# Four attention blocks on one core: where the values of an earlier half stand in TensorE's order

## The chip, the cores and the metric

The kernel runs on one core of a Trainium2 chip. The time is that of the device for one execution, in microseconds (us); 374.49 us is the median of three runs of the kernel before.

## The reference

An activation `x` of 8 batches x 128 positions x 128 channels goes through four cross-attention layers one after the other, against one context of 8 x 128 x 256. Layers 0 and 3 are "narrow" (RMS norm, 16 query heads of 8 dimensions that share 4 key and value heads, no mask). Layers 1 and 2 are "wide" (16 heads of 64 dimensions, a bias on some columns). Everything is float32. Cut to a wide layer:

```python
q = hidden_states @ Wq                      # per batch 128 x 1024, 16 heads of 64
k = encoder_hidden_states @ Wk
v = encoder_hidden_states @ Wv
logits = einsum('bhqd,bhkd->bhqk', q, k) * scale + col_bias
probs = softmax(logits, axis=-1)
out = einsum('bhqk,bhkd->bhqd', probs, v)
out = out.reshape(B, HW, 1024) @ Wo + bo + hidden_states
```

## The kernel before

A **job** `n` is one layer of one batch; there are 32 (`JOBS`), in two turns of 16: four batches through layers 0, 1, 2, 3, then the other four. Jobs 4 to 11 and 20 to 27 are wide, the rest narrow. A job has two **halves** of 8 heads, `h` = 0 and 1, and all engines count halves by `o = 2n + h`; "half 50" is `o` = 50, the first half of job 25. Within a half the heads are on two sides of four heads each.

The kernel is software-pipelined over a loop of half slots. Each engine has its own program in a fixed order written out by hand, and semaphores tie them together; no scheduler moves anything. In the slot of half `o` TensorE (PE) does, in this order:

1. the **scores** of half `o` (`wide_scores`, line 834): 8 products with a 64-row contraction, two at a time on the upper and the lower 64 rows, into the banks `scores_ps`;
2. the **values** of half `o-3` (`weighted_values`, line 881): 8 products that give 64 rows each, two at a time on two column halves of the array, into `v_ps`, from the transposed probabilities `probsT`;
3. the **transposes** of the probabilities of half `o-2` (`transpose_probs`, line 847) into `pt_ps`;
4. **fills**: projections of the context into keys and values that a later job needs (`project_context`, lines 700 to 702). The table `FILLS` says which half slot has how many; slots 12 to 22, 44, 46, 48, 50, 52 and 54 have one or two, the odd slots 49 and 51 have none, slot 53 has a small one;
5. the **queries** of half `h` of the next job (`queries`, line 786) into `q_ps`, or, where the next job is narrow and `h` is 0, its mean square and queries (`narrow_queries`, lines 799 and 806), which write into `v_ps` and so wait for `v_read`, VectorE's copy of the values two jobs back out of that bank;
6. with `h` = 0 the **output projection** of job `n-2` (line 899), 8 products of the values of both its halves with `Wo`, into `v_ps` too, after the same `v_read`.

VectorE (DVE) in the slot of half `o` goes: with `h` = 1 the residual add of job `n-2` (line 633); the scores of half `o` out of PSUM with the bias and the row minimum, side 0, then side 1 (line 596), with a reciprocal between them; the values of half `o-3` out (`oT`, line 623); the transposed probabilities of half `o-2` out, both sides (`probsT`, line 616, semaphores `pt_read`); a reciprocal. ScalarE (ACT) does the exponentials of half `o` (line 476) and copies out queries and fills; GpSimd (POOL) multiplies with the reciprocals (line 376).

The values of half `o-3` wait on TensorE for `pt_read` of half `o-3` of both sides, that is for the last two copies of VectorE's slot `o-1`, and for `v_read`:

```python
if n > 0:
    pe.wait_ge(v_read, uses(n, h) - 1)
...
for side in range(2):
    pe.wait_ge(pt_read[side], o + 1)
```

Of the kernel before, what the change touches and what calls it, by code (L numbers as in the profile page):

```python
# [103 lines left out]
def job(n):  # L104

    return JOBS[n] if 0 <= n < NJOBS else (None, None)


def is_narrow(n):

    return 0 <= n < NJOBS and JOBS[n][0] in NARROW


def is_wide(n):

    return 0 <= n < NJOBS and JOBS[n][0] not in NARROW


def uses(n, h):

    return sum(2 if is_wide(m) else 1 for m in range(n)) + (h + 1 if is_wide(n) else 1)
# [29 lines left out]
def count_of(bank, use):  # L151

    return BANK_USES[bank].index(use) + 1


def narrow_index(n):

    return NARROW_JOBS.index(n)


def build(nc, xT, ctxT, narrow_w, narrow_kv, kv_w, qo_w, small, tokens, outT):
    with ExitStack() as ctx:
# [108 lines left out]
        def valid(o):  # L271

            return 0 <= o < 2 * NJOBS
# [422 lines left out]
        def _(pe):  # L696
# [81 lines left out]
            def queries(n, h):  # L778

                l, b = job(n)  # L780
                free_bank(Q0, ("queries", n, h))
                pe.wait_ge(qo_loaded[l - 1], 16)
                pe.wait_ge(y_read, JOBS.index((l - 1, b)) + 1)
                for c in range(4):
                    first = WQ + (4 * h + c) * P
                    last = nc.tensor.matmul(q_ps[:, c * T:(c + 1) * T], w_qo[:, l - 1, first:first + P], x[:, b, :],  # L786
                                            start=True, stop=True)
                last.then_inc(bank_full[Q0], 1)
# [19 lines left out]
            def narrow_scores(n):  # L808

                i = narrow_index(n)  # L810
                for r in range(REP):
                    free_bank(r, (2 * n + r // 2, r % 2))
                pe.wait_ge(kd_made, i + 1)
                pe.wait_ge(qn_made, i + 1)
                for r in range(REP):
                    rows = slice(PART * r, PART * (r + 1))
                    nc.tensor.matmul(banks[r][:], qn[rows, n % 2, :], kd[rows, i % KD_RING].rearrange("p g k -> p (g k)"),  # L817
                                     start=True, stop=True).then_inc(bank_full[r], 1)

            def wide_scores(n, h):  # L820
                o = 2 * n + h
                l, b = job(n)
                for side in range(2):
                    free_bank(side, (o, side))
                pe.wait_ge(bank_read[Q0], count_of(Q0, ("queries", n, h)))
                f = WIDE_ROWS.index((b // 2, l))
                for m in (2 * h, 2 * h + 1):
                    name = f"k{f}.{m}"
                    pe.wait_ge(bank_read[FILL_BANK[name]], count_of(FILL_BANK[name], name))

                for c in range(4):
                    for side in range(2):
                        rows = slice(side * WIDE_D, (side + 1) * WIDE_D)
                        last = nc.tensor.matmul(banks[side][:, c * S:(c + 1) * S], qT[rows, 4 * h + c, :],  # L834
                                                kT[rows, f % KV_RING, 4 * h + c, b % 2 * S:(b % 2 + 1) * S],
                                                start=True, stop=True)
                        if c == 3:
                            last.then_inc(bank_full[side], 1)

            def transpose_probs(o):  # L840
                for side in range(2):
                    pe.wait_ge(probs_made[side], o + 1)
                    if o > 0:
                        pe.wait_ge(pt_read[side], o)
                    for q in range(4):
                        cols = slice(q * S, (q + 1) * S)
                        last = nc.tensor.transpose(pt_ps[side][:, cols], probs[:, o % PROBS_RING, side, cols], identity)  # L847
                    last.then_inc(pt_full[side], 1)

            def weighted_values(n, h):  # L850
                o = 2 * n + h
                l, b = job(n)
                if l in NARROW and h == 0:
                    return
                if n > 0:
                    pe.wait_ge(v_read, uses(n, h) - 1)
                if n > 0 and (h == 0 or l in NARROW):
                    pe.wait_ge(y_read, n)
                if is_narrow((o + 4) // 2):
                    pe.wait_ge(rms_out, narrow_index((o + 4) // 2) + 1)  # L860
                    pe.wait_ge(qn_made, narrow_index((o + 4) // 2) + 1)
                for side in range(2):
                    pe.wait_ge(pt_read[side], o + 1)
                if l in NARROW:
                    i = narrow_index(n)
                    pe.wait_ge(vn_made, i + 1)
                    for g in range(KV_HEADS):
                        for r in range(REP):
                            last = nc.tensor.matmul(v_ps[PART * r:PART * (r + 1), 0:T],  # L869
                                                    v_narrow[:, i % 2, PART * g:PART * (g + 1)],  # L870
                                                    probsT[:, (o - 1 + r // 2) % PROBST_RING, r % 2, g * T:(g + 1) * T], start=(g == 0),
                                                    stop=(g == KV_HEADS - 1))
                    last.then_inc(v_full, 1)
                    return
                f = WIDE_ROWS.index((b // 2, l))
                name = f"v{f}.{2 * (b % 2) + h}"
                pe.wait_ge(bank_read[FILL_BANK[name]], count_of(FILL_BANK[name], name))
                for c in range(4):
                    for side in range(2):
                        head = 8 * h + 2 * c + side  # L880
                        last = nc.tensor.matmul(  # L881
                            v_ps[side * WIDE_D:(side + 1) * WIDE_D, c * T:(c + 1) * T],
                            v[:, f % KV_RING, b % 2, head * WIDE_D:(head + 1) * WIDE_D],
                            probsT[:, o % PROBST_RING, side, c * T:(c + 1) * T], start=True, stop=True)
                last.then_inc(v_full, 1)
# [16 lines left out]

            def half(n, h):
                o = 2 * n + h
                if is_wide(n):
                    wide_scores(n, h)
                if is_narrow(n) and h == 0:
                    narrow_scores(n)
                if o == 0:
                    warm_up(3)  # L910
                if o >= FIRST_WAIT and valid(o - 2) and o - 2 != LAST:
                    pe.wait_ge(bank_read[Q0], len(BANK_USES[Q0]))
                    warm_up(4, q_ps)
                if valid(o - 3) and is_wide((o - 3) // 2):
                    weighted_values((o - 3) // 2, (o - 3) % 2)
                if valid(o - 2) and o - 2 != LAST:
                    transpose_probs(o - 2)
                if valid(o - 3) and is_narrow((o - 3) // 2):
                    weighted_values((o - 3) // 2, (o - 3) % 2)
                names = [name for name, bank in FILLS.get(o, [])]  # L920
                behind = names[1:] if h == 0 and is_narrow(n) and is_narrow(n + 1) else []
                for name in names[:len(names) - len(behind)]:
                    project_context(name)
                if is_wide(n + 1):
                    queries(n + 1, h)
                if h == 0 and is_narrow(n + 1):
                    narrow_queries(n + 1)
                if o - 1 == LAST:
                    transpose_probs(LAST)
                if h == 0 and n >= 2:  # L930
                    output_projection(n - 2)
                for name in behind:
                    project_context(name)

            def warm_up(count, bank=pt_ps[0]):

                for _ in range(count):
                    nc.tensor.matmul(bank[:, 0:T], mean_w[:], mean_w[:], start=True, stop=True)  # L938
# [8 lines left out]
            for n, h in HALVES:  # L947
                half(n, h)
# [59 lines left out]
```

## Time and profile before

| | |
|---|---|
| median of 3 runs | 374.49 us (374.46 to 374.75) |
| the profiled execution's own time | 374.53 us |
| its span, first to last instruction | 372.7 us |
| busy: TensorE, ScalarE, VectorE, GpSimd | 358.1, 280.1, 249.1, 178.7 us |
| mean granted TensorE clock | 0.986 of full speed |

The span is 1.8 us shorter than the profiled execution's time. Weight loads (PEld) and matmuls (PE) are shown apart. A float32 matmul stands as two instructions in the trace, so that the 8 products of the scores or the values of a half are x16, and the 4 of the queries x8; a transpose stands as two too, 4 on a side. A matmul's end is modelled and pipelined with the next one's start, so starts are compared with starts here.

### The profile page before, as it was taken

To read this page: it belongs to the slowest core of one execution; us is meant where nothing else is said; L and a number is where in the kernel's file an instruction comes from. 1 tells how busy PE (TensorE), PEld (TensorE's weight loads), DVE (VectorE), ACT (ScalarE), POOL (GpSimd) and SP (SyncE) were. 2 spreads that over 40 slices of the span, in tenths; PEclk is the share of its full clock that TensorE was granted. 3 is DMA by queue.
4 is the path that set the end of the run, shared out by engine and by line. 5 is a ranking of instruction groups with operands and counts; after the bars stand their busy time and mean duration, and the time that the engine had idled before them with its cause. 6 is when DMAs were issued, how large, how long until landed. Compare 5 with 4: busy or idle time off the path is not lost.

```text
span 372.7 us, 10531 instructions
## 1 busy us (share of the span) xinstructions
PE 358.1 (96%) x3552; PEld 311.1 (83%) x3552; DVE 249.1 (67%) x1385; ACT 280.1 (75%) x1176; POOL 178.7 (48%) x205
## 2 busy tenths in 40 slices
PE   8897999999999999999999999999999999988985
PEld 7776779889989989978887878988999999866874
DVE  2899675365465466579677777556647666689884
ACT  4897897865755756576899999987667666676893
POOL 3696643552332334265667665433233424456761
PEclk9897899999999999999999999999999999999999
DMA  7943000000000000000000000000000000000000
GB/s 229 409 144 139 0 4 3 2 1 2 3 2 0 3 2 2 1 2 3 2 11 7 9 11 2 3 2 2 2 2 3 3 0 3 2 3 0 3 9 21
DMA packets 4883, 9.71 MB, mean 26 GB/s; under 512 B 608, under 2 KB 3296, under 8 KB 4576
## 3 DMA queue, kind: packets, MB, share of 16 engines
q1 hardware_dynamic: 4400, 8.65, 6.5%
q8 instruction: 29, 0.48, 0.5%
q10 hardware_dynamic: 432, 0.40, 0.4%
q14 instruction: 22, 0.18, 0.2%
HBM read 8.53 MB, written 0.52 MB: 24 GB/s over the span
## 4 chain that ended last, share of the span: by engine, by line
PE 86%; DVE 10%; ACT 2%; issue 1%; POOL 0%; DVEq 0%; POOLq 0%
PE pt_ps L847 14%; PE scores_ps L834 9%; PE v_ps L899 9%; PE v_ps L881 8%; PE q_ps L786 7%; DVE probs L596 5%; PE fill_ps L700 5%; PE fill_ps L701 5%; PE fill_ps L702 5%; PE v_ps L869 4%; PE scores_ps L817 4%; PE scores_ps L700 3%; PE scores_ps L702 2%; PE scores_ps L701 2%; PE pt_ps L938 1%; PE q_ps L700 1%
## 5 line engine op out<-in xcount | busy, mean ns | idle before, releaser
L476 ACT ACTIVATE probs<-probs,negmax 128x128 f32<-128x128 f32 x512 | 198.4, 390 | 64.8 <-DVE negmax L596 64.5
L376 POOL TENSOR_TENSOR probs<-probs,inv 128x512 f32<-128x512 f32 x127 | 135.1, 1063 | 178.0 <-DVE inv L603 177.8
L476 ACT ACTIVATION_READ_ACCUMULATOR probs<-probs,negmax 128x1 f32 x512 | 96.8, 189 | 0.0
L596 DVE CUSTOM_DVE_ANT_0 probs<-scores_ps,col_bias 128x128 f32<-128x128 f32 x256 | 58.2, 283 | 39.3 <-PE scores_ps L834 39.3
L847 PE MATMUL pt_ps<-smalls,probs 128*128 128x128 f32 x512 | 69.6, 279 | 0.7 <-DVE probsT L616 0.7
L847 PEld LDWEIGHTS pt_ps<-smalls,probs 128*128 128x128 f32 x512 | 56.2, 142 | 15.2 <-issue 12.4
L616 DVE COPY probsT<-pt_ps 128x512 f32<-128x512 f32 x96 | 62.7, 680 | 2.7 <-PE pt_ps L847 2.6
L596 DVE CUSTOM_DVE_ANT_0 probs<-scores_ps,no_bias,inv_rms 128x128 f32<-128x128 f32 x128 | 36.7, 342 | 12.9 <-PE scores_ps L817 12.9
L596 DVE DVE_READ_ACCUMULATOR2_ANT negmax<- 128x1 f32 x512 | 41.9, 82 | 0.0
L834 PE MATMUL scores_ps<-kT,qT 64*128 64x128 f32 x512 | 37.2, 285 | 0.0
L596 DVE CUSTOM_DVE_ANT_0 probs<-fill_ps,no_bias,inv_rms 128x128 f32<-128x128 f32 x128 | 36.4, 339 | 0.0
L881 PE MATMUL v_ps<-probsT,v 128*64 128x128 f32 x512 | 35.0, 279 | 1.0 <-DVE rms L573 1.0
L834 PEld LDWEIGHTS scores_ps<-kT,qT 64*128 64x128 f32 x512 | 31.1, 187 | 3.9
L786 PE MATMUL q_ps<-x,w_qo 128*128 128x128 f32 x256 | 33.8, 275 | 0.0
L786 PEld LDWEIGHTS q_ps<-x,w_qo 128*128 128x128 f32 x256 | 32.0, 191 | 1.3 <-issue 0.2
L881 PEld LDWEIGHTS v_ps<-probsT,v 128*64 128x64 f32 x512 | 27.3, 136 | 6.8 <-issue 3.4
L899 PE MATMUL v_ps<-oT,w_qo 128*128 128x128 f32 x256 | 31.2, 275 | 0.0
L633 DVE SCALAR_TENSOR_TENSOR x<-v_ps,smalls,x 128x128 f32<-128x128 f32 x16 | 5.6, 350 | 36.5 <-PE v_ps L899 36.5
L899 PEld LDWEIGHTS v_ps<-oT,w_qo 128*128 128x128 f32 x256 | 29.9, 192 | 0.0
L603 DVE RECIPROCAL inv<-rowsum 128x4 f32<-128x4 f32 x128 | 21.9, 171 | 11.6 <-ACT probs L476 11.6
L467 ACT ACTIVATE qT<-q_ps 128x512 f32<-128x512 f32 x32 | 18.7, 586 | 9.0 <-PE q_ps L786 9.0
L623 DVE COPY oT<-v_ps 128x512 f32<-128x512 f32 x32 | 21.9, 685 | 0.0
(146 smaller groups left out, 642.6 us busy)
## 6 DMA issues: line engine op xcount, KB each, us to landing
kT<-in_kv_w SPq DMA_DIRECT2D x6, 512.0 KB, 6.2
w_qo<-in_qo_w SPq DMA_DIRECT2D x2, 1024.0 KB, 8.2
v<-in_ctxT SPq DMA_DIRECT2D x4, 256.0 KB, 9.2
v<-in_kv_w SPq DMA_DIRECT2D x2, 512.0 KB, 10.8
outT<-x SPq DMA_DIRECT2D x8, 64.0 KB, 1.6
x<-in_xT SPq DMA_DIRECT2D x1, 384.0 KB, 7.6
oT<-in_narrow_kv ACTq DMA_DIRECT2D x1, 320.0 KB, 4.0
wn<-in_narrow_w SPq DMA_DIRECT2D x2, 64.0 KB, 5.1
```

The lines of the kernel that those rows point to most:

```text
L376: nc.gpsimd.tensor_tensor(p4, p4, inv[:, o % 2, side, :].unsqueeze(2).broadcast_to([P, 4, S]), ALU.mult,).then_inc(probs_made[side], 1)
L476: last = nc.scalar.activation(e, e, ACT.Exp, scale=-1.0, bias=negmax[:, o % 2, side, q:q + 1], accum_out=rowsum[:, o % 2, side, q:q + 1])
L596: last = nc.vector.tensor_tensor_reduce(out=probs[:, o % PROBS_RING, side, cols], in0=banks[bank][:, cols], in1=bias, scale=scale, scalar= ...
L616: nc.vector.tensor_copy(probsT[:, o % PROBST_RING, side, :], pt_ps[side][:]).then_inc(pt_read[side], 1)
L700: nc.tensor.matmul(out, a_hi, b_hi, start=(n == 0), stop=False)
L701: nc.tensor.matmul(out, a_lo, b_hi, start=False, stop=False)
L702: last = nc.tensor.matmul(out, a_hi, b_lo, start=False, stop=(n == len(moving) - 1))
L786: last = nc.tensor.matmul(q_ps[:, c * T:(c + 1) * T], w_qo[:, l - 1, first:first + P], x[:, b, :], start=True, stop=True)
L834: last = nc.tensor.matmul(banks[side][:, c * S:(c + 1) * S], qT[rows, 4 * h + c, :], kT[rows, f % KV_RING, 4 * h + c, b % 2 * S:(b % 2 + 1 ...
L847: last = nc.tensor.transpose(pt_ps[side][:, cols], probs[:, o % PROBS_RING, side, cols], identity)
L881: last = nc.tensor.matmul(v_ps[side * WIDE_D:(side + 1) * WIDE_D, c * T:(c + 1) * T], v[:, f % KV_RING, b % 2, head * WIDE_D:(head + 1) * ...
L899: last = nc.tensor.matmul(y_ps, w, oT[:, c, :], start=(c == 0), stop=(c == (1 if l in NARROW else IC) - 1))
```

## The change

In a slot with `h` = 0 of a wide job, where half `o-3` is wide too, the values of half `o-3` are made ahead of the scores of half `o`. That is so in the slots 12, 14, 16, 18, 20, 22 and 44, 46, 48, 50, 52, 54: twelve. All other slots keep their order; no instruction is added or removed.

```diff
             def half(n, h):
                 o = 2 * n + h
+                values_first = is_wide(n) and h == 0 and valid(o - 3) and is_wide((o - 3) // 2)
+                if values_first:
+                    weighted_values((o - 3) // 2, (o - 3) % 2)
                 if is_wide(n):
                     wide_scores(n, h)
                 if is_narrow(n) and h == 0:
...
-                if valid(o - 3) and is_wide((o - 3) // 2):
+                if valid(o - 3) and is_wide((o - 3) // 2) and not values_first:
                     weighted_values((o - 3) // 2, (o - 3) % 2)
                 if valid(o - 2) and o - 2 != LAST:
                     transpose_probs(o - 2)
```

On TensorE at the border of slots 49 and 50, before: the queries that end slot 49, then scores of half 50, values of half 47, transposes of half 48. (`bank_read_0` and `_1` tell that the two score banks are read, `bank_read_4` that `q_ps` is.)

```order
L786 MATMUL q_ps<-x,w_qo 128x128 [waits y_read,qo_loaded_1,bank_read_4]
L786 MATMUL q_ps<-x,w_qo 128x128 x3
L834 MATMUL scores_ps<-kT,qT 128x128 [waits bank_read_4,bank_read_0,bank_read_1]
L834 MATMUL scores_ps<-kT,qT 128x128 x7
L881 MATMUL v_ps<-probsT,v 64x128 [waits pt_read_1,bank_read_1,pt_read_0,v_read]
L881 MATMUL v_ps<-probsT,v 64x128 x7
L847 MATMUL pt_ps<-smalls,probs 128x128 [waits pt_read_0,probs_made_0]
```

The same place in the changed kernel:

```order
L786 MATMUL q_ps<-x,w_qo 128x128 [waits y_read,qo_loaded_1,bank_read_4]
L786 MATMUL q_ps<-x,w_qo 128x128 x3
L881 MATMUL v_ps<-probsT,v 64x128 [waits pt_read_1,bank_read_1,pt_read_0,v_read]
L881 MATMUL v_ps<-probsT,v 64x128 x7
L834 MATMUL scores_ps<-kT,qT 128x128 [waits bank_read_4,bank_read_0,bank_read_1]
L834 MATMUL scores_ps<-kT,qT 128x128 x7
L847 MATMUL pt_ps<-smalls,probs 128x128 [waits pt_read_0,probs_made_0]
```

The wait for `pt_read`, which had the scores ahead of it, now stands right behind the queries, and the scores stand behind that wait.

On TensorE in slot 54, from the scores to the output projection, before (the rows between are the transposes and a fill):

```order
L834 MATMUL scores_ps<-kT,qT 128x128 [waits bank_read_2,bank_read_4,bank_read_3,bank_read_1,bank_read_0]
L834 MATMUL scores_ps<-kT,qT 128x128 x7
L881 MATMUL v_ps<-probsT,v 64x128 [waits pt_read_1,bank_read_3,pt_read_0,v_read]
L881 MATMUL v_ps<-probsT,v 64x128 x7
...
L799 MATMUL v_ps<-mean_w,x_sq 128x2 [waits qn_made,sq_ready,rms_out,v_read]
L806 MATMUL v_ps<-x,wn 128x128 [waits norms_folded,y_read]
L899 MATMUL v_ps<-oT,w_qo 128x128 [waits v_read]
```

The same place in the changed kernel:

```order
L881 MATMUL v_ps<-probsT,v 64x128 [waits pt_read_1,bank_read_3,pt_read_0,v_read]
L881 MATMUL v_ps<-probsT,v 64x128 x7
L834 MATMUL scores_ps<-kT,qT 128x128 [waits bank_read_2,bank_read_4,bank_read_3,bank_read_1,bank_read_0]
L834 MATMUL scores_ps<-kT,qT 128x128 x7
...
L799 MATMUL v_ps<-mean_w,x_sq 128x2 [waits qn_made,sq_ready,rms_out,v_read]
L806 MATMUL v_ps<-x,wn 128x128 [waits norms_folded,y_read]
L899 MATMUL v_ps<-oT,w_qo 128x128 [waits v_read]
```

Between the scores and line 799, whose `v_read` VectorE gives only after it has copied out the scores, there are now eight products fewer.

## Rows read from the trace of the kernel before

**Rows 1.** The page: busy time by engine; the chain that ended last, by engine.

```profile
PE 358.1 (96%) x3552; PEld 311.1 (83%) x3552; DVE 249.1 (67%) x1385; ACT 280.1 (75%) x1176; POOL 178.7 (48%) x205
...
PE 86%; DVE 10%; ACT 2%; issue 1%; POOL 0%; DVEq 0%; POOLq 0%
```

**Rows 2.** Busy time by stretch: us, then PE, PEld, DVE, ACT, POOL; clock.

```profile
325.00:350.00 25.00, 22.70 (x214) 17.95 (x215) 21.08 (x116) 17.33 (x83) 15.86 (x21) 1.00 0.01 1
```

**Rows 3.** Timeline of PE, slots 49 and 50: start us, took us, what.

```profile
290.79 1.16 PE L834 MATMUL scores_ps<-kT,qT 64*128 64x128 f32 x16
291.88 1.09 PE L881 MATMUL v_ps<-probsT,v 128*64 128x128 f32 x16
292.91 1.09 PE L847 MATMUL pt_ps<-smalls,probs 128*128 128x128 f32 x8
293.84 1.06 PE L786 MATMUL q_ps<-x,w_qo 128*128 128x128 f32 x8
294.83 1.16 PE L834 MATMUL scores_ps<-kT,qT 64*128 64x128 f32 x16
...
299.28 1.05 PE L786 MATMUL q_ps<-x,w_qo 128*128 128x128 f32 x8
300.17 1.95 PE L899 MATMUL v_ps<-oT,w_qo 128*128 128x128 f32 x16
```

**Rows 4.** Timeline of DVE, slot 49, in brackets idle time and its releaser.

```profile
291.99 0.29 DVE L596 CUSTOM_DVE_ANT_0 probs<-scores_ps,col_bias 128x128 f32<-128x128 f32 x1 [0.73 <-PE scores_ps L834]
...
294.35 1.28 DVE L616 COPY probsT<-pt_ps 128x512 f32<-128x512 f32 x2
```

**Rows 5.** Timeline: last copies of DVE's slot 53, start of PE's slot 54.

```profile
316.86 1.27 DVE L616 COPY probsT<-pt_ps 128x512 f32<-128x512 f32 x2
...
318.05 1.16 PE L834 MATMUL scores_ps<-kT,qT 64*128 64x128 f32 x16
```

**Rows 6.** Timeline: last copies of DVE's slot 13, start of PE's slot 14.

```profile
92.30 1.28 DVE L616 COPY probsT<-pt_ps 128x512 f32<-128x512 f32 x2
...
94.19 1.16 PE L834 MATMUL scores_ps<-kT,qT 64*128 64x128 f32 x16
```

**Rows 7.** Timeline of slot 54: values copied out, narrow mean square, output projection.

```profile
321.00 0.69 DVE L623 COPY oT<-v_ps 128x512 f32<-128x512 f32 x1
...
322.27 0.42 PEld L799 LDWEIGHTS v_ps<-mean_w,x_sq 128*128 128x128 f32 x2
...
322.94 1.95 PE L899 MATMUL v_ps<-oT,w_qo 128*128 128x128 f32 x16
```

**Rows 8.** Timeline of slot 56, where the narrow mean square waits for such a copy.

```profile
332.88 0.68 DVE L623 COPY oT<-v_ps 128x512 f32<-128x512 f32 x1
...
333.62 0.30 PEld L799 LDWEIGHTS v_ps<-mean_w,x_sq 128*128 128x128 f32 x2 [1.30 <-DVE oT L623]
...
334.17 1.95 PE L899 MATMUL v_ps<-oT,w_qo 128*128 128x128 f32 x16
```

**Rows 9.** Timeline of PE: scores straight before transposes; warm-up before values, before transposes.

```profile
237.38 1.16 PE L834 MATMUL scores_ps<-kT,qT 64*128 64x128 f32 x16
238.48 1.09 PE L847 MATMUL pt_ps<-smalls,probs 128*128 128x128 f32 x8
...
340.43 1.16 PE L938 MATMUL q_ps<-mean_w 128*128 128x128 f32 x8
341.52 1.09 PE L881 MATMUL v_ps<-probsT,v 128*64 128x128 f32 x16
...
349.01 1.16 PE L938 MATMUL q_ps<-mean_w 128*128 128x128 f32 x8
350.01 1.04 PE L847 MATMUL pt_ps<-smalls,probs 128*128 128x128 f32 x8
```

**Rows 10.** Timeline of slot 57: a copy of DVE, and values on PEld that wait.

```profile
336.49 0.28 DVE L579 TENSOR_SCALAR qn<-v_ps 128x128 f32<-128x128 f32 x1
...
337.05 0.88 PEld L881 LDWEIGHTS v_ps<-probsT,v 128*64 128x64 f32 x16 [1.13 <-issue]
```

## The prediction

> **What bounds the kernel now.** I read the page first: TensorE is busy for 96% of the span, and the chain that ended last runs on it for 86% [rows 1]. So a microsecond that TensorE loses in the wide slots is nearly a microsecond of the kernel, and work of the other engines counts only where TensorE waits for it. Then the timeline of TensorE over two slots [rows 3]. The reader is to see that the groups stand shoulder to shoulder: scores 290.79, values 291.88, transposes 292.91, queries 293.84, the next scores 294.83. No wait stands between queries, scores and values, so the change has no wait to remove; it can gain only if a changed neighbour makes a group cheaper. Last, the timeline of VectorE, to see when what the values need is ready. Its slot 49 begins with the scores of half 49: it idles 0.73 us for them, starts at 291.99, which is 1.20 us after TensorE began those scores, and then works without a gap to the end of its two probsT copies at 294.35 + 1.28 = 295.63 [rows 3, 4]. Thus the copies end 4.84 us after the scores of an odd slot begin, and how much time TensorE takes until the next even slot depends on the fills in between.
>
> **Nothing removed, one block moved.** In twelve slots 8 products of the values go ahead of 8 products of the scores. No other engine's program changes. Three effects follow.
>
> *1. Neighbours.* Before, the even slot goes queries, scores, values, transposes; after, queries, values, scores, transposes. From start to start, before: queries to scores 0.99, scores to values 1.09, values to transposes 1.03 us [rows 3], 3.11 in all. After, queries to values: four warm-up products of the shape of four query products take 1.09 to values and 1.00 to transposes [rows 9], so values come in 0.09 dearer than transposes do; queries take 0.99 to scores and 0.89 to an output projection [rows 3], 0.10 dearer. So values are entered at the price of scores: 0.99. Scores to transposes stands in the trace: 238.48 - 237.38 = 1.10 [rows 9], as scores to values. Values to scores, call it d, stands nowhere. The nearest row is values to transposes, 1.03; since scores cost the same before values as before transposes, I take it that the next group does not matter and use d = 1.02 to 1.03, and the slot is 3.11 as before: 0 us. The bounds: below, 8 products at the pace of four queries, which are as many columns in the 8 instructions that 16 take in pairs, 0.89 [rows 3]; above, 1.03 plus the 0.10 by which scores are entered dearer, 1.13. That is -0.13 to +0.10 us in each of twelve slots, -1.6 to +1.2.
>
> What these rows show is a loss at each change of the tile's form (64*128, 128*64, 128*128): values take 1.03 and 0.89 is their pace. The Trainium skill, TensorEngine Tiling (Array Packing), section Tiling Modes, says that changing the tiling mode drains the array. Another of its pages, TensorE: Matmul & The Clock Gate, Part 2 (step by step), says that weight loads are pulled ahead of running matmuls where the row groups don't conflict. By the first there are three drains before and three after and the sum below stands, 377.4; by the second, taken at its word, the losses would go, which is the rival with 373.0 below.
>
> *2. The values wait for VectorE.* They now want to start where the scores started. In slot 14 that is 94.19, the copies end at 92.30 + 1.28 = 93.58, and 0.61 us are left over [rows 6]; slots 16, 18, 20, 46 and 48 repeat this, and slots 12, 22 and 44, behind larger fills, have more. Nothing is lost in these nine. Slot 50 follows a slot without a fill: the start is wanted at 294.83, the copies end at 295.63, 0.80 late [rows 3, 4]. Slot 52 repeats it. Slot 54 follows a small fill: wanted 318.05, copies end 316.86 + 1.27 = 318.13, 0.08 late [rows 5]. To this comes the time from a copy's end to the waiting weight load: 0.06 in one row (332.88 + 0.68 = 333.56 to 333.62 [rows 8]), 0.28 for values themselves (336.49 + 0.28 = 336.77 to 337.05 [rows 10]). I take 0.15, between the two and nearer the first, whose wait is for a plain copy too. The stalls: 0.95 + 0.95 + 0.23 = 2.13 us; with 0.06 it is 1.86, with 0.28 it is 2.52. Behind the waiting values stand the scores of the same half, and everything VectorE, ScalarE and GpSimd then do waits for those; before, the scores filled this very time. VectorE's chain hangs on the scores of the odd slot, which the stall shifts too, so slot 50's delay doesn't shorten slot 52's.
>
> *3. The scores are d = 1.02 later in the even slot,* and VectorE with them, since it waits for scores at the start of each slot. Its copy of the values (oT) in that slot comes 1.02 later. The output projection needs it. The copy ends as the probsT copies begin, 294.35 - 290.79 = 3.56 us after the scores' start, now 4.58 after their old start; with a fill and queries before it the projection starts 300.17 - 294.83 = 5.34 after it [rows 3, 4], with 0.76 to spare. In slots 22 and 54 the next job is narrow, and the mean square of line 799, which needs the same copy, stands ahead of it. In slot 54 the copy ends at 321.00 + 0.69 = 321.69; its weight load began at 322.27 [rows 7]. After: 321.69 + 1.02 = 322.71, plus 0.06 is 322.77, and from such a released load to the output projection it is 334.17 - 333.62 = 0.55 [rows 8], so 323.32 against 322.94 [rows 7]: 0.38 late. Slot 22 repeats it, the two 0.76 us. This term moves with d.
>
> What else the late scores touch has cover. Exponentials, query copy and fill copy of ScalarE end 1 us later in the even slots, but the next scores out come 4 us after that. The probabilities of side 1 are released by a reciprocal that stands in VectorE's next slot behind scores that aren't late, so the transposes two slots on don't notice. If that cover were gone, each even slot would lose up to 1.02.
>
> **The sum.** 0 + 2.13 + 0.76 = 2.9 us. The profiled execution took 374.53, which is the median of 374.49 within 0.04; 374.53 + 2.9 = 377.4 us. With d = 0.89 it is 1.6 less (375.9), with wake-ups of 0.06 besides 375.6; with d = 1.13 it is 1.2 more, and with wake-ups of 0.28 besides 379.0.
>
> **The rivals.**
> *Faster: all three changes of form become free.* If weights were loaded ahead across each of them, the losses above would go: 0.10 into the values, 0.13 out of them, 1.09 - 0.89 = 0.20 out of the scores, 0.43 per slot. Eight slots give 8 x 0.43 = 3.44; in slots 50 and 52 the start is fixed by VectorE and 0.95 - 0.33 = 0.62 is lost in each; slot 54 loses 0.61 - 0.13 = 0.48, slot 22 0.38 - 0.23 = 0.15. In all -1.6: 372.9 to 373.0. With a share f of these prices gone the change is 2.9 - 4.5 f, so f must be over 0.8 for a gain of 0.2%. Against it: scores to transposes, one of the three, is in the trace already at its full 1.10 [rows 9]. 4 in 100.
> *Only d is cheap (0.89):* still slower, 375.6 to 375.9. The next pair could start on rows or columns that are idle; but values to transposes shows no such thing. 11 in 100.
> *The loss is taken up later.* From 325 to 350 us TensorE idles 25.00 - 22.70 = 2.30 us at an unchanged clock of 1.00 [rows 2]. If these waits were for something that doesn't move, 2.9 - 2.3 = 0.6 would be left, 375.1, which is no change. Against it: the one that is shown there waits for a VectorE copy [rows 8], and that follows from the scores just delayed. 8 in 100.
> *More waits than I count:* the 0.61 of the six slots like 14 is used up, from copies more than 0.3 later on; each 0.1 beyond that costs 0.6, over 379. 5 in 100.
> *The sum holds:* 376.2 to 379.0, 72 in 100.
>
> **How the numbers follow.** A measurement of this kernel tells 0.2% (0.75 us) from no change. The likeliest case gives 377.4. The range 375.6 to 379.0 is that of the unknown prices and takes in the case of the cheap d; outside lie the other three, 17 in 100. Slower: 72 + 11 + 5 = 88; within 0.2%: 8; faster: 4.
>
> **What would show it.** In the trace after, values of the even slots should start 0.9 us behind the end of the queries in slots 50 and 52, with TensorE idle and VectorE's line 616 named as the releaser, and 0.2 in slot 54; nowhere else. Values to scores reads d directly, near 1.03. Line 799 in slots 22 and 54 should wait for the oT copy of line 623. The scores' start to the transposes' start reads 1.10. I am wrong if d is far from 1.03, if the values of slots 14 to 20 wait too, or if the idle time after 325 us shrinks by what was lost before. A granted clock below 1.00 behind the new stalls would be a cost that no row here has: TensorE's 1.30 us without a weight load in slot 56 [rows 8] lies in a stretch at 1.00 [rows 2], and these stalls are shorter.

## The result, and the profile after

The changed kernel takes 377.58 us (median of 12 runs, 376.01 to 378.06); the kernel before, timed beside it 12 times, 374.49 us. The ratio is 1.0082, with a 95% interval of 1.0065 to 1.0099: 3.1 us slower, between 2.4 and 3.7. The forecast was 377.4 us, in a range of 375.6 to 379.0.

The page, busy time by engine and then the chain by engine, against [rows 1]:

```profile
PE 359.2 (96%) x3552; PEld 311.0 (83%) x3552; DVE 249.0 (66%) x1385; ACT 280.1 (74%) x1176; POOL 178.5 (47%) x205
...
PE 81%; DVE 15%; issue 1%; DMA 1%; SPq 0%; ACT 0%; POOL 0%; DVEq 0%; POOLq 0%
```

No engine does more work to speak of, but the chain now runs through VectorE for 15% of the span instead of 10%. The chain of waits (engine and line, waited for: us in all, times, longest) says where it has come in:

```profile
DVE probs L596 <- PE scores_ps L834: 54.1, 32, 4.1
...
PEld v_ps L799 <- DVE oT L623: 2.7, 4, 1.3
...
PE v_ps L881 <- DVE probsT L616: 2.2, 3, 1.0
```

The last line is new: the values wait three times for the copies of the transposed probabilities. The mean square of line 799 now waits four times for the oT copy; before it was twice:

```profile
PEld v_ps L799 <- DVE oT L623: 1.6, 2, 1.3
```

Here are slots 49 and 50 on TensorE, against [rows 3] (start us, took us, what, idle time and releaser):

```profile
291.38 1.16 PE L834 MATMUL scores_ps<-kT,qT 64*128 64x128 f32 x16
292.47 1.09 PE L881 MATMUL v_ps<-probsT,v 128*64 128x128 f32 x16
293.49 1.09 PE L847 MATMUL pt_ps<-smalls,probs 128*128 128x128 f32 x8
294.42 1.06 PE L786 MATMUL q_ps<-x,w_qo 128*128 128x128 f32 x8
296.46 1.09 PE L881 MATMUL v_ps<-probsT,v 128*64 128x128 f32 x16 [0.98 <-DVE probsT L616]
297.49 1.16 PE L834 MATMUL scores_ps<-kT,qT 64*128 64x128 f32 x16
298.58 1.09 PE L847 MATMUL pt_ps<-smalls,probs 128*128 128x128 f32 x8
```

and VectorE's copies that the values wait for, against [rows 4]:

```profile
294.93 1.28 DVE L616 COPY probsT<-pt_ps 128x512 f32<-128x512 f32 x2
```

The copies end at 296.21, 4.83 us after the scores of slot 49 began, as before. The values could have followed the queries by 0.98 (slot 14, below), at 295.40; they start at 296.46, 1.06 late. Values to scores is 1.03, scores to transposes 1.09. Slot 52 reads the same (queries 306.73, values 308.77). In slot 54 the values are 0.34 late (319.74 + 0.99 = 320.73, start 321.07), and the mean square of line 799 waits, against [rows 7]:

```profile
321.07 1.09 PE L881 MATMUL v_ps<-probsT,v 128*64 128x128 f32 x16 [0.28 <-DVE probsT L616]
...
325.05 0.69 DVE L623 COPY oT<-v_ps 128x512 f32<-128x512 f32 x1
...
325.79 0.30 PEld L799 LDWEIGHTS v_ps<-mean_w,x_sq 128*128 128x128 f32 x2 [0.54 <-DVE oT L623]
...
326.34 1.95 PE L899 MATMUL v_ps<-oT,w_qo 128*128 128x128 f32 x16
```

From that slot's transposes (323.19) to its output projection it is now 3.15 us; before it was 322.94 - 320.16 = 2.78. So 0.37 is lost, and in slot 22 as much (152.16 to 155.31, before 151.93 to 154.71). In a slot with room nothing waits; slot 14, where before the scores followed the queries [rows 6]:

```profile
93.46 1.05 PE L786 MATMUL q_ps<-x,w_qo 128*128 128x128 f32 x8
94.44 1.09 PE L881 MATMUL v_ps<-probsT,v 128*64 128x128 f32 x16
95.46 1.16 PE L834 MATMUL scores_ps<-kT,qT 64*128 64x128 f32 x16
96.56 1.09 PE L847 MATMUL pt_ps<-smalls,probs 128*128 128x128 f32 x8
```

Queries to transposes is 3.10 us here, and 3.10 before (93.21 to 96.31).

Up to slot 8 the traces differ by up to 3.3 us even where the programs are equal there (its scores start between 52.0 and 55.4 us), and the end differs too. So I compare a stretch that holds all the edits: from the start of the scores of slot 8 to the start of the transposes in slot 56. The granted clock is 1.00 from 55.5 to 330 us in all these traces but that of values first in the odd slots. The last column is for the timed runs. They fall in two groups by TensorE's mean granted clock, 0.993 and more or 0.991 and less, and the kernel before takes 1.2 to 1.5 us longer in the second. So each group's median is set against the same group of the kernel before that was timed on the same chip; the clocks of the kernel before beside the changed kernel's first twelve runs are not known.

| kernel | scores, slot 8 | transposes, slot 56 | stretch | against before | timed, higher and lower clock |
|---|---|---|---|---|---|
| before | 53.70 | 331.46 | 277.76 | | |
| changed | 53.95 | 334.86 | 280.91 | +3.15 | not known |
| values first in eight slots with room | 53.29 | 331.04 | 277.75 | -0.01 | -0.1, -0.3 |
| only in slots 50, 52 | 53.66 | 333.55 | 279.89 | +2.13 | +2.2, +2.2 |
| only in slots 22, 54 | 53.37 | 332.19 | 278.82 | +1.06 | +1.1, +0.7 |
| changed, filler of four | 53.81 | 334.76 | 280.95 | +3.19 | none, +4.3 |
| order of before, filler of four | 54.06 | 333.61 | 279.55 | +1.79 | +3.2, +3.1 |
| changed, fills moved | 52.33 | 332.88 | 280.55 | +2.79 | +2.8, +2.9 |
| order of before, fills moved | 53.92 | 331.68 | 277.76 | 0.00 | -0.3, +0.1 |
| values first in odd slots too | 52.48 | 351.89 | 299.41 | +21.65 | none, +19.9 (one run) |
| changed, filler of five | 55.35 | 336.41 | 281.06 | +3.30 | +2.9 (one run), +4.8 |
| changed, again | 52.04 | 332.96 | 280.92 | +3.16 | +2.9, +3.2 |

### The profile page after: what moved, and what is told of

Read it like the earlier page. It is cut to its first block, busy times and chain, and to the rows that moved or that the text cites. A ratio compares the mean times of both kernels' runs of the same rounds, so it can differ in the third digit from the quotient of the medians.

```text
span 376.1 us, 10531 instructions
## 1 busy us (share of the span) xinstructions
PE 359.2 (96%) x3552; PEld 311.0 (83%) x3552; DVE 249.0 (66%) x1385; ACT 280.1 (74%) x1176; POOL 178.5 (47%) x205
## 4 chain that ended last, share of the span: by engine, by line
PE 81%; DVE 15%; issue 1%; DMA 1%; SPq 0%; ACT 0%; POOL 0%; DVEq 0%; POOLq 0%
PE pt_ps L847 13%; PE scores_ps L834 9%; PE v_ps L899 8%; DVE probs L596 8%; PE v_ps L881 7%; PE q_ps L786 7%; PE fill_ps L700 5%; PE fill_ps L701 4%; PE fill_ps L702 4%; PE scores_ps L817 4%; PE v_ps L869 4%; PE scores_ps L700 3%; PE scores_ps L702 2%; PE scores_ps L701 2%; DVE probsT L616 2%
```

## The experiments

The first four ran on one chip, where the kernel before took 374.38 us.

**Slots with room.** The edit:

```diff
-                values_first = is_wide(n) and h == 0 and valid(o - 3) and is_wide((o - 3) // 2)
+                values_first = o in (12, 14, 16, 18, 20, 44, 46, 48)
```

> Values first only in the eight slots 12, 14, 16, 18, 20, 44, 46 and 48, where the copies that the values need end before the values' turn. Theory (the loss is three stalls of the values and two of the narrow mean square): 0.0 us against the kernel before, within 0.2 of it by the span from slot 8 to slot 56. Rival (each swapped slot pays for another order of the tile forms): eight twelfths of what isn't a stall; if all of the 3.1 us were such a price, +2.1 us.

Measured: 373.50 us, ratio 0.9994 (0.9965 to 1.0023), and -0.01 us by the stretch. Eight swaps cost nothing and give nothing; slot 48 of this kernel:

```profile
282.15 1.05 PE L786 MATMUL q_ps<-x,w_qo 128*128 128x128 f32 x8
283.14 1.09 PE L881 MATMUL v_ps<-probsT,v 128*64 128x128 f32 x16
284.16 1.16 PE L834 MATMUL scores_ps<-kT,qT 64*128 64x128 f32 x16
285.25 1.09 PE L847 MATMUL pt_ps<-smalls,probs 128*128 128x128 f32 x8
```

The rival of a price per swapped slot falls.

**Slots behind a slot without a fill.** The same line with `o in (50, 52)`.

> Values first only in slots 50 and 52, which stand behind slots without a fill. Theory: both values stall 1.05 us as in the changed kernel, +2.1 us against the kernel before, and TensorE shows 0.98 us of idle time twice, released by the probsT copy. Rival (a price per swapped slot): two twelfths of 3.1 us, +0.5 us.

Measured: 375.42 us, ratio 1.0048 (1.0025 to 1.0072), +2.13 us by the stretch. Its chain of waits:

```profile
PE v_ps L881 <- DVE probsT L616: 2.0, 2, 1.0
```

Two stalls of 1.0 are all of it. The medians of all runs are only 1.04 us apart because six of these ten runs are of the higher clock and most of those of the kernel before (14 of 25) of the lower; within each group it is +2.2 (table).

**Slots before a narrow job.** The same line with `o in (22, 54)`.

> Values first only in slots 22 and 54, whose next job is narrow. Theory: 0.37 us in each for the mean square that waits for the oT copy, and 0.34 us for the values of slot 54: +1.1 us against the kernel before. Rival (a price per swapped slot): +0.5 us.

Measured: 375.21 us, ratio 1.0039 (1.0013 to 1.0065), +1.06 us by the stretch. The values of slot 54 wait once for the probsT copies, and line 799 waits for the oT copy four times in the kernel, twice as often as with the eight slots alone:

```profile
PEld v_ps L799 <- DVE oT L623: 2.7, 4, 1.3
...
PE v_ps L881 <- DVE probsT L616: 0.3, 1, 0.3
```

The three parts, -0.01 + 2.13 + 1.06 = 3.18, give the whole, 3.15.

**Work in the place of the stall.** To the changed kernel, behind the fills of the slots 49 and 51:

```diff
+                if o in (49, 51):
+                    spare, name = (B0, "k7.2") if o == 49 else (B1, "k7.3")
+                    pe.wait_ge(bank_read[spare], count_of(spare, name))
+                    warm_up(4, banks[spare])
                 if is_wide(n + 1):
                     queries(n + 1, h)
```

> The changed kernel, with four more float32 matmuls of 128 columns (0.89 us, into a bank that nobody reads) behind the transposes in each of the slots 49 and 51, 1.78 us of added work on TensorE. Theory: the filler fills the time in which the values of slots 50 and 52 waited, the stalls fall from 1.05 to 0.16 us, and the time stays within 0.3 us of the changed kernel. Rival (TensorE isn't waiting there but working more dearly): +1.8 us against the changed kernel.

Measured by the stretch: +3.19 us against before, 0.04 against the changed kernel. The filler is free where it stands; values follow the queries by 1.15 instead of 2.04:

```profile
294.28 1.06 PE L945 MATMUL fill_ps<-mean_w 128*128 128x128 f32 x8
295.17 1.06 PE L786 MATMUL q_ps<-x,w_qo 128*128 128x128 f32 x8
296.32 1.09 PE L881 MATMUL v_ps<-probsT,v 128*64 128x128 f32 x16
```

But the time is 378.90 us (four runs, ratio 1.0154, 1.0113 to 1.0195), 1.3 more than the changed kernel takes on this chip in runs of the lower clock (377.6, two runs, the last experiment), and that isn't in the stretch. In this execution 1.1 of it lies behind the last instruction of VectorE: that ends at 374.03 and the span at 377.1, 3.1 us later; before it is 370.73 and 372.7, 2.0, and in the changed kernel 2.0 too.

**The same filler in the order of before.** These four ran on another chip, where the kernel before took 374.17 us.

```diff
-                values_first = is_wide(n) and h == 0 and valid(o - 3) and is_wide((o - 3) // 2)
+                values_first = False
```

> The order of before in all slots, with the same filler as the run before this one (four matmuls, 0.89 us, in each of the slots 49 and 51). Theory: nothing waits there, so the filler is paid in full: +1.8 us against the kernel before. Rival (the filler is free in any order, and says nothing on the stall): 0.

Measured: +1.79 us by the stretch, what 2 x 0.89 makes. So the filler is paid in full in the old order and free in the new. The time is 376.43 us, ratio 1.0083 (1.0056 to 1.0109), and here too the profiled execution is longer outside the stretch, 3.7 us from VectorE's last instruction (372.87) to the end (376.6). Within each group of runs it is +3.1 to +3.2, some 1.4 more than the stretch has.

**Fills moved, with the change.**

```diff
-    46: [("k7.1", B1)], 47: [("k7.2", B0)], 48: [("k7.3", B1)], 50: [("v7.0", B0)], 52: [("v7.1", B1)],
+    46: [("k7.1", B1)], 47: [("k7.2", B0)], 48: [("k7.3", B1)], 49: [("v7.0", B0)], 51: [("v7.1", B1)],
```

> The changed kernel with the fill of slot 50 moved to slot 49 and that of slot 52 to slot 51. Theory: the values of slots 50 and 52 no longer wait, but now nothing but the queries stands between the transposes and the output projection of these slots, which needs the oT copy of VectorE 3.56 + 1.02 us after the old start of the scores: it waits some 0.8 us in each. With 1.1 us for slots 22 and 54 that is +2.7 us against the kernel before, 0.5 less than the change. Rival (the loss is only where the values wait for their copies): +1.1 us.

Measured: 376.15 us, ratio 1.0075 (1.0050 to 1.0099), +2.79 us by the stretch. The stall is gone from the values and stands ahead of the output projection:

```profile
298.23 1.06 PE L786 MATMUL q_ps<-x,w_qo 128*128 128x128 f32 x8
299.90 2.05 PE L899 MATMUL v_ps<-oT,w_qo 128*128 128x128 f32 x16 [0.61 <-DVE oT L623]
301.89 1.16 PE L834 MATMUL scores_ps<-kT,qT 64*128 64x128 f32 x16
```

Behind the queries the projection would start 0.89 later, at 299.12; it is 0.78 late, and takes 1.99 to the scores, 0.1 more than where it doesn't wait (301.81 to 303.69 in the changed kernel). The fill that the odd slot gets, the even slot lacks, and the late scores need cover in both places.

**Fills moved, order of before.** The same table, with `values_first = False`.

> The order of before in all slots, with the two fills moved as in the run before this one. Theory: the output projections of slots 50 and 52 start 3.9 us after the scores, when the oT copy has ended (3.56 us), and nothing waits: 0.0 us against the kernel before. Rival (moving the fills costs by itself, through their banks or their copies on ScalarE): what the moved fills cost is seen here, and the run with the change and moved fills has to be read against it.

Measured: 374.48 us, ratio 1.0002 (0.9982 to 1.0022), 0.00 us by the stretch. Moving the fills costs nothing by itself; the old order has room for both tables.

**Values first in the odd slots too.**

```diff
-                values_first = is_wide(n) and h == 0 and valid(o - 3) and is_wide((o - 3) // 2)
+                values_first = is_wide(n) and valid(o - 3) and is_wide((o - 3) // 2)
```

> Values first in the odd slots of the wide jobs as well. Theory: there the values wait for the residual add, which waits for the output projection just ahead, some 0.7 us in each of fourteen slots, and the odd scores are then 1.7 us later, so that the copies for the next even slot come too late in most of them: 10 us and more over the kernel before, my estimate +18 us. Rival (values first is a matter of room for the probsT copies alone): the odd slots have 1 us of room or more behind them, and the time stays near that of the changed kernel.

Measured: 394.47 us in its one run, 20.3 over the kernel before, and +21.65 us by the stretch; I had estimated 18. Slot 13, the residual add between the projection and the values:

```profile
86.14 1.95 PE L899 MATMUL v_ps<-oT,w_qo 128*128 128x128 f32 x16
88.13 0.35 DVE L633 SCALAR_TENSOR_TENSOR x<-v_ps,smalls,x 128x128 f32<-128x128 f32 x1 [2.80 <-PE v_ps L899]
...
88.58 1.09 PE L881 MATMUL v_ps<-probsT,v 128*64 128x128 f32 x16 [0.49 <-issue]
```

The values start 0.10 us after the add ends (88.48). The profile names no releaser there, but the program makes these values wait for the add. Slot 14's values then wait 0.60 us for the probsT copies, which slot 14 of the changed kernel does not. In the whole kernel:

```profile
PE v_ps L881 <- DVE probsT L616: 9.8, 11, 2.0
PE v_ps L881 <- issue: 5.3, 11, 0.5
```

These waits are 15.1 of the 21.65 us. Another 1.5 us is a cost of the clock that no other trace of the table has. Behind a wait of 2.01 us in slot 50 the granted clock fell to 0.50, the lower level of 1.2 GHz, from about 308.2 to 311.5 us:

```profile
307.24 1.12 PE L881 MATMUL v_ps<-probsT,v 128*64 128x128 f32 x16 [2.01 <-DVE probsT L616]
308.29 2.08 PE L834 MATMUL scores_ps<-kT,qT 64*128 64x128 f32 x16
310.30 1.69 PE L847 MATMUL pt_ps<-smalls,probs 128*128 128x128 f32 x8
```

Scores and transposes took 3.46 us there (308.29 to 311.75) and 1.94 in slot 52 (323.70 to 325.64), where the same wait of 2.01 us left the clock at 1.00.

**Five filler matmuls, and the changed kernel again.** On the first chip again, where the kernel before now took 374.25 us, the filler had `warm_up(5, ...)`; beside it ran the changed kernel as it is.

> The changed kernel with five filler matmuls (1.12 us) instead of four in each of the slots 49 and 51: a little more than the 1.05 us by which the values of slots 50 and 52 were late. Theory: no wait is left before these values, and the filler costs 2 x (1.12 - 1.05) = 0.1 us against the changed kernel run beside it. The run with four fillers took 1.3 us longer by its few timed runs, though from slot 8 to slot 56 its trace was only 0.04 us longer. Rival (the filler has a price outside the slots where it stands): this run is over 1 us slower than the changed kernel too.

> The changed kernel once more, on the same chip as the run with five fillers, so that the two can be compared: +3.1 us against the kernel before.

Measured: 379.22 us with five (six runs, ratio 1.0117, 1.0073 to 1.0160), 376.30 us for the changed kernel (nine runs, ratio 1.0062, 1.0041 to 1.0083). By the stretch the five cost 281.06 - 280.92 = 0.14 us, as expected, and no wait for the copies is left in slots 50 and 52. The rest of the 2.9 us lies outside. Some of it is the clock: seven of the nine runs of the changed kernel are of the higher one, and one of the six with the filler. Among the runs of the lower clock it is 379.27 (five runs) against 377.63 (two), 1.6 us; the one run of the higher clock, 376.24, is no slower than the changed kernel's 376.18.

In the profiled execution the rest stands ahead of slot 8 (55.35 against 52.04) and not at the end. Half of these 3.3 us the kernel before has too (53.70): from 30 to 40 us its granted clock is 0.66, as with this filler (0.67), and 0.83 in the changed kernel's trace. The other half begins with an input that came late. TensorE waits for it as in no other trace, and is 1.4 us behind the kernel before by the first fill that needs VectorE's w_lo (16.78 against 15.33):

```profile
5.90 2.05 PE L737 MATMUL q_ps<-v,oT 128*128 128x256 f32 x4 [0.67 <-DMA v<-in_ctxT]
```

So by the timed runs the rival is right in part: in most of their runs the filler kernels pay 1.1 to 1.5 us outside the stretch. All three of them load their instructions in 30 packets on one queue where the others do in 29; whether that is the cause was not tried, and it stays open. It doesn't touch the verdict on the stall, which rests on the stretch.

## Why the prediction was right

**The bound.** TensorE without a gap through the wide slots was read rightly: every delay of TensorE there arrives at the end of the stretch, to 0.03 us in the sum of the three parts, and the two filler matmul groups in the old order cost just their own length.

**Neighbours, 0 us.** The changed kernel has 0.98 + 1.02 + 1.10 = 3.10 in slot 14, the kernel before 3.10 too (the prediction's rows gave 3.11), and the eight swapped slots alone give -0.01 us. The open price d is 1.02 to 1.03, the value chosen; the two bounds, 0.89 and 1.13, weren't reached. What carried it was the row of scores before transposes [rows 9]: a group in tiles costs the same whatever comes next. The Trainium skill, TensorEngine Tiling (Array Packing), section Tiling Modes, says that a change of the tiling mode drains the array. The trace agrees as far as it goes: three changes before, three after, and 3.10 us both times; that the loss at each is a drain, no row shows. At these changes the weight loads start with their matmuls or 0.01 us ahead (94.44, 95.46 and 96.55 us in slot 14), where those of the queries start 0.12 ahead (93.34 and 93.46). The Trainium skill, TensorE: Matmul & The Clock Gate, Part 2, has weight loads pulled ahead where the row groups don't conflict. This case doesn't test that: at each change one of the two groups uses all 128 rows, so the row groups do conflict, and the prediction's rival took the rule beyond its condition.

**The values' wait, 2.13 us.** In the three slots named and in no other. It measured 1.06 + 1.06 + 0.34 = 2.46. The term that was off is the wake-up: I took 0.15 from the copy's end to the start, and it is 296.46 - 296.21 = 0.25 in each of the three. The row for the values themselves had said 0.28 [rows 10]; the one for line 799 (0.06) [rows 8] was the wrong one to lean to.

**The mean square, 0.76 us.** 0.37 in each of slots 22 and 54, 0.74. Together 0 + 2.46 + 0.74 = 3.20 where 2.9 was forecast and 3.15 measured.

**Cover.** The forecast took the delay of the other engines in the even slots for hidden. Moving the fills shows how near the edge that was for the output projection: with the fill it had 0.76 us to spare by my count (0.68 in the changed kernel's trace, from the copy's end at 301.13 to 301.81); without it, it was 0.78 late.

**The rivals.** Cheap changes of form fall, all of them and d alone. The loss was not taken up later: the idle times of TensorE in slots 56 and 57, which [rows 2] hold, are still there:

```profile
337.02 0.38 PE L799 MATMUL v_ps<-mean_w,x_sq 128*128 128x2 f32 x2 [1.06 <-DVE oT L623]
...
340.49 1.09 PE L881 MATMUL v_ps<-probsT,v 128*64 128x128 f32 x16 [0.97 <-DVE rms L573]
```

They follow from the scores that had been delayed. No further slot waited. The clock stayed at its full level (2.4 GHz) behind the stalls, as from 325 to 350 us after:

```profile
325.00:350.00 25.00, 22.60 (x210) 18.16 (x210) 20.60 (x109) 17.56 (x86) 14.11 (x18) 1.00 0.00 1
```

## What to carry to other kernels

When the bounding engine runs without a gap, swapping two of its blocks can gain only through what they cost as neighbours; first look whether the one that moves up is ready by then, slot by slot, because the room depends on what fills the slot before. The block that moves down is delayed by the other's full length, and so is everything that other engines make of it: follow that to the next place where the bounding engine needs one of those results. A piece of independent work put in the place of a supposed stall tells a stall from dearer work: it is free in the one case and paid in full in the other.

## What the runs showed of the hardware that I had not expected

The order of two groups of matmuls in different tile forms (64*128 and 128*64) between full ones makes no difference: eight swaps changed the stretch by 0.01 us. From the end of a VectorE copy to a waiting group of values it takes 0.25 us on TensorE (0.22 to its weight load, at 296.43), but to the weight load of the waiting mean square only 325.79 - 325.74 = 0.05; why they differ was not tried. Behind one wait of 2.01 us TensorE's clock was at 1.2 GHz for some 3 us, behind another as long, in the same execution, it stayed at 2.4 GHz. And kernels with a few more matmuls took 1.1 to 1.5 us longer at their start or end in most of their timed runs, away from where those matmuls stand; the cause is open.
